# Attention's row-sum reciprocals on VectorE one unit later, without the round trip through memory, and key and value fetches moved into the first half of units

## The reference, cut to what matters

```python
h = _ada_ln(x, cond, Wln1, bln1)
q, k, v = heads(h @ Wq + bq), heads(h @ Wk + bk), heads(h @ Wv + bv)   # 16 heads of 32
scores = einsum('bhqd,bhkd->bhqk', q, k) / sqrt(32)
attn = softmax(scores, axis=-1)
x = x + einsum('bhqk,bhkd->bhqd', attn, v) @ Wo + bo
h = _ada_ln(x, cond, Wln2, bln2)
x = x + gelu(h @ W1 + b1) @ W2 + b2
```

## Time and profile before

| what | value |
|---|---|
| median of 3 runs | 3295.89 us (3295.88 to 3303.61) |
| the profiled execution's own time | 3315.78 us |
| its span, first to last instruction | 3314.2 us |
| mean granted TensorE clock | 0.978 |
| busy share of the span | PE 97%, DVE 63%, POOL 43%, ACT 42% |
| attention | about 378 to 2014 us, 32 units |

### The profile page before, as it was taken

How to read it: one execution, slowest core, us unless ns; L and a number is a source line. 1 busy time by engine, 2 the same in 40 slices (tenths; PEclk the granted TensorE clock), 3 DMA queues, 4 the chain that set the end, 5 groups by cost and what they waited for, 6 DMA issues and landing times.

```text
span 3314.2 us, 44368 instructions
## 1 busy us (share of the span) xinstructions
PE 3211.7 (97%) x16890; PEld 2200.4 (66%) x16890; DVE 2079.5 (63%) x3537; ACT 1391.1 (42%) x2703; POOL 1436.7 (43%) x656
## 2 busy tenths in 40 slices
PE   8798999999999999999999998899999999999999
PEld 7686655555555555555555545688888888778888
DVE  4647778778788787787878775543333332226766
ACT  2121366666666566665666663221111111012222
POOL 0200478778787786776867763210000000002222
PEclk9899999999999999999999999999999999889999
DMA  5474488888988788797887877520111112201221
GB/s 195 143 221 141 142 196 199 183 187 191 205 180 199 186 186 199 174 205 183 186 200 171 193 175 214 197 92 15 39 38 39 39 39 79 77 22 64 73 78 58
DMA packets 185883, 464.12 MB, mean 140 GB/s; under 512 B 27164, under 2 KB 69276, under 8 KB 154183
## 3 DMA queue, kind: packets, MB, share of 16 engines
q0 software_dynamic: 31968, 232.80, 31.5%
q1 hardware_dynamic: 153703, 228.49, 23.3%
HBM read 151.90 MB, written 75.76 MB: 69 GB/s over the span
## 4 chain that ended last, share of the span: by engine, by line
PE 86%; DMA 7%; DVE 3%; issue 2%; ACT 1%; POOL 1%; SPq 1%; DVEq 0%; POOLq 0%; ACTq 0%
PE ps L372 13%; PE ps L647 13%; PE ps L659 12%; PE ps L1178 11%; PE ps L1165 11%; DMA accd<-pt 5%; PE ps L446 4%; PE ps L1712 4%; PE ps L665 3%; PE ps L1725 3%; PE ps L450 2%; PE ps L1746 1%; PE ps L1541 1%; PE ps L1029 1%; DMA ao<-ao_d 1%
## 5 line engine op out<-in xcount | busy, mean ns | idle before, releaser
L385 DVE TENSOR_REDUCE nmp<-ps 128x1 f32<-128x512 f32 x1966 | 1202.2, 680 | 169.5 <-PE ps L372 168.1
L716 ACT ACTIVATE pt<-ps 128x512 f32<-128x512 f32 x2048 | 1033.4, 627 | 556.6 <-PE ps L647 556.5
L822 POOL TENSOR_TENSOR pacc<-pacc,pt 128x2048 f32<-128x2048 f32 x186 | 882.1, 4742 | 37.7 <-ACT pt L716 32.7
L647 PE MATMUL ps<-qs,ks 128*128 128x512 f32 x2048 | 817.3, 403 | 4.4 <-issue 4.0
L372 PE MATMUL ps<-ks,qs 96*128 96x512 f32 x1966 | 811.5, 413 | 3.3 <-POOL ones L798 3.3
L372 PEld LDWEIGHTS ps<-ks,qs 96*128 96x128 f32 x1966 | 377.8, 192 | 271.0 <-DVE nmp L385 162.7
L659 PE MATMUL ps<-pt,vq 128*32 128x512 f32 x4096 | 492.5, 598 | 0.0
L647 PEld LDWEIGHTS ps<-qs,ks 128*128 128x128 f32 x2048 | 393.8, 193 | 99.6 <-ACT pt L716 16.6
L1165 PE MATMUL ps<-hpb,w 128*128 128x512 f32 x1536 | 382.8, 399 | 3.4 <-DMA x_d<-x 3.4
L1178 PE MATMUL ps<-w,gp 128*128 128x512 f32 x1536 | 380.5, 396 | 2.3 <-DVE gp L1314 2.3
L1178 PEld LDWEIGHTS ps<-w,gp 128*128 128x128 f32 x1536 | 289.4, 188 | 71.7 <-DVE gp L1314 2.8
(11 more groups left out here) (175 smaller groups left out, 3180.9 us busy)
## 6 DMA issues: line engine op xcount, KB each, us to landing
accd<-pt POOLq DMA_DIRECT2D x222, 1024.0 KB, 9.1
qk_d<-st SPq DMA_DIRECT2D x128, 256.0 KB, 2.7
ks<-qk_d SPq DMA_DIRECT2D x24, 1024.0 KB, 16.0
qs<-qk_d SPq DMA_DIRECT2D x96, 256.0 KB, 6.8
xina<-in_x SPq DMA_DIRECT2D x8, 1024.0 KB, 6.4
v_d<-vst SPq DMA_DIRECT2D x32, 256.0 KB, 2.3
vq<-v_d SPq DMA_DIRECT2D x8, 1024.0 KB, 14.0
recb<-r_d SPq DMA_DIRECT2D x32, 256.0 KB
```

Of the source, the lines that this page charges most:

```text
L385: dve.tensor_reduce(nmp[:, n // 4, n % 4:n % 4 + 1], ps[:, ring.bank["max", u], :], AX.X, ALU.max, negate=True).then_inc(s_mr, 1)
L647: pe.matmul(ps[:, score_bank(n), :], ksb[w % 2][:, hh, 128 * kt:128 * kt + 128], qsb[:, v % 3, hh, :], start=True, stop=True).then_inc(s_s ...
L716: act.activation(pt[:, g % 8, hh, :], ps[:, score_bank(n), :], ACT.Exp, scale=SCALE).then_inc(s_exp, 1)
L822: pool.tensor_tensor(pacc[:, :, :], first, pt[:, g % 8, :, :], ALU.add).then_inc(s_add, 1)
```

## The change

The reciprocal's way through memory is taken out: sp_fold_sums, sp_store_recip, sp_load_recip, the tiles rs and rr and the buffer r_d are gone. VectorE copies the repeated sums of 128 x 512 to accs, which has two buffers, and takes the reciprocal of all 128 x 512 in place, one unit later: at the end of step 0 of unit v for unit v - 2. GpSimd multiplies behind its tile 2 of unit v, and SP stores at step 3. accv has two buffers too. In the last unit, unit 30's reciprocal is at step 3, its multiplication behind tile 10, and its store at step 6; unit 31's reciprocal stays at t = 2 of the output projection.

The keys are fetched in six DMAs of 512 KB in place of three of 1 MB, at steps 1, 3 and 4 of chunks 0 and 1, each held until the unit's scores have come to that step. The queries go out at step 2 under a wait that holds them until the scores of that step (before, they went out as soon as SP came to them). The values are fetched at step 4 of chunk 2, from a v_d whose layout now gives each partition one contiguous piece of 8 KB; the stores to v_d write pieces of 512 bytes where they wrote 2 KB. In the output projection x2 becomes one tile of five buffers, aT and boB lie elsewhere, and one wait for the end of attention is gone.

```diff
@@ -161,9 +161,8 @@
-    v_d = nc.dram_tensor("v_d", [B * S, D], F32, kind="Internal").ap()
+    v_d = nc.dram_tensor("v_d", [4 * B, 128, S // 128, 128], F32, kind="Internal").ap()
     ao_d = nc.dram_tensor("ao_d", [NT, 128, D], F32, kind="Internal").ap()
-    r_d = nc.dram_tensor("r_d", [2, 4, CH], F32, kind="Internal").ap()
...
-        accv = take("accv", [128, CH])
-        recb = take("recb", [128, CH])
+        accv = take("accv", [128, 2, CH])
+        accs = take("accs", [128, 2, CH])
         ones = take("ones", [128, 32])
-        rs = take("rs", [128, 16])
-        rr = take("rr", [128, 16])
...
-                pe.wait_ge(s_kd[w % 2], 48 * (w // 2 + 1))
+                pe.wait_ge(s_kd[w % 2], 96 * (w // 2 + 1))
...
 
-        def sp_load_k(w, r):
-            b, f, part = w // 4, 128 * (w % 4), (2, 3, 2)[r]
-            sp.dma_start(ksb[w % 2][32 * r:32 * r + 32, :, :].bitcast(F32),
-                         qk_d[b, part, f:f + 128, :].rearrange("(h e) s -> e h s", e=HD)).then_inc(s_kd[w % 2], 16)
+        def sp_load_k(w, r, half):
+
+            b, f, part = w // 4, 128 * (w % 4) + 64 * half, (2, 3, 2)[r]
+            sp.dma_start(ksb[w % 2][32 * r:32 * r + 32, 2 * half:2 * half + 2, :].bitcast(F32),
+                         qk_d[b, part, f:f + 64, :].rearrange("(h e) s -> e h s", e=HD)).then_inc(s_kd[w % 2], 16)
...
@@ -586,7 +584,8 @@
                             sp.wait_ge(s_qst[r], 128)
                         sp.wait_ge(s_pad, 3)
                     if ci == NCH and j in (1, 3, 5):
-                        sp_load_k(0, j // 2)
+                        sp_load_k(0, j // 2, 0)
+                        sp_load_k(0, j // 2, 1)
                     if ci == NCH and j in (6, 7):
                         sp_load_q(j - 6)
                     if ci == NCH + 2 and j == 0:
...
                     else:
-                        rows0 = CH * ci + 128 * (j - 8)
                         sp.wait_ge(s_vev, 4 * ci + j - 7)
-                        sp.dma_start(v_d[rows0:rows0 + 128, :], vst[:, j - 8, :]).then_inc(s_vst[j - 8], 16)
+                        sp.dma_start(v_d[4 * b:4 * b + 4, :, 4 * c + j - 8, :].rearrange("w p e -> p w e"),
+                                     vst[:, j - 8, :].rearrange("p (w e) -> p w e", w=4)).then_inc(s_vst[j - 8], 16)
...
@@ -717,9 +716,9 @@
 
         def act_values(v):
             act.wait_ge(s_pv, 16 * v + 16)
-            if v:
-                act.wait_ge(s_an, v)
-            act.activation(accv[:, :], ps[:, 7, :], ACT.Copy).then_inc(s_accv, 1)
+            if v >= 2:
+                act.wait_ge(s_an, v - 1)
+            act.activation(accv[:, v % 2, :], ps[:, 7, :], ACT.Copy).then_inc(s_accv, 1)
 
         def act_attention():
             qkv_over(act)
@@ -735,9 +734,13 @@
 
         def dve_sums(v):
             dve.wait_ge(s_end, v + 1)
-            if v:
-                dve.wait_ge(s_ao, 16 * v)
-            dve.tensor_copy(recb[:, :], ps[:, ring.bank["sums", v], :]).then_inc(s_accs, 1)
+            if v >= 2:
+                dve.wait_ge(s_ao, 16 * (v - 1))
+            dve.tensor_copy(accs[:, v % 2, :], ps[:, ring.bank["sums", v], :]).then_inc(s_accs, 1)
+
+        def dve_recip(v):
+            dve.wait_ge(s_accs, v + 1)
+            dve.reciprocal(accs[:, v % 2, :], accs[:, v % 2, :]).then_inc(s_rec, 1)
 
         def dve_add(kt):
 
@@ -755,12 +758,6 @@
             dve.wait_ge(s_wo, 16)
             dve.tensor_copy(wo[:, 0, k, :], wtmpo[:, k, :]).then_inc(s_wh, 1)
             dve_split(12 + k, wo[:, 1, k, :], wtmpo[:, k, :], wo[:, 0, k, :])
-
-        def dve_recip(v):
-            dve.wait_ge(s_rsd, 16 * (v + 1))
-            if v:
-                dve.wait_ge(s_rw, 16 * v)
-            dve.reciprocal(rr[:, :], rs[:, :]).then_inc(s_rec, 1)
 
         def dve_attention():
             qkv_over(dve)
@@ -779,7 +776,9 @@
                         dve_max(u)
                         if u % 64 == 63:
                             dve_row_max(u // 64)
-                if f == 2 and v:
+                if f == 0 and v >= 2:
+                    dve_recip(v - 2)
+                if f == 3 and v == NU - 1:
                     dve_recip(v - 1)
                 if v == NU - 1:
                     for kt in (2 * f, 2 * f + 1):
@@ -789,9 +788,9 @@
                         dve_out_turn(f - 5)
 
         def pool_values(v):
-            pool.wait_ge(s_recb, 16 * (v + 1))
+            pool.wait_ge(s_rec, v + 1)
             pool.wait_ge(s_accv, v + 1)
-            pool.tensor_tensor(recb[:, :], accv[:, :], recb[:, :], ALU.mult).then_inc(s_an, 1)
+            pool.tensor_tensor(accs[:, v % 2, :], accv[:, v % 2, :], accs[:, v % 2, :], ALU.mult).then_inc(s_an, 1)
 
         def pool_attention():
             qkv_over(pool)
@@ -820,39 +819,23 @@
                         pool.wait_ge(s_add, add_count(v, kt) - 1)
                         first = pacc[:, :, :]
                     pool.tensor_tensor(pacc[:, :, :], first, pt[:, g % 8, :, :], ALU.add).then_inc(s_add, 1)
-                if kt == 9 and v:
+                if kt == 2 and v >= 2:
+                    pool_values(v - 2)
+                if kt == 10 and v == NU - 1:
                     pool_values(v - 1)
 
         def sp_load_v(w):
-            b, f = w // 4, 128 * (w % 4)
-            sp.dma_start(vq[:, w % 2, :, :],
-                         v_d[S * b:S * b + S, f:f + 128].rearrange("(t p) e -> p t e", p=128)).then_inc(s_vq[w % 2], 16)
-
-        def sp_fold_sums(v):
-
-            sp.wait_ge(s_accs, v + 1)
-            if v:
-                sp.wait_ge(s_rec, v)
-            sp.dma_start(rs[:, :], recb[0:128:32, :].rearrange("h (c i) -> h c i", i=16)).then_inc(s_rsd, 16)
-
-        def sp_store_recip(v):
-            sp.wait_ge(s_rec, v + 1)
-            if v >= 2:
-                sp.wait_ge(s_recb, 16 * (v - 1))
-            sp.dma_start(r_d[v % 2].rearrange("h (c i) -> (h c) i", i=16), rr[:, :]).then_inc(s_rw, 16)
-
-        def sp_load_recip(v):
-
-            sp.wait_ge(s_rw, 16 * (v + 1))
-            sp.dma_start(recb[:, :], r_d[v % 2].unsqueeze(1).to_broadcast([4, 32, CH])).then_inc(s_recb, 16)
+            sp.dma_start(vq[:, w % 2, :, :], v_d[w]).then_inc(s_vq[w % 2], 16)
 
         def sp_store_ao(v):
             w, qc = divmod(v, NCH)
             b, k = divmod(w, 4)
             t0 = 16 * b + 4 * qc
             sp.wait_ge(s_an, v + 1)
+            if v:
+                sp.wait_ge(s_ao, 16 * v)
             sp.dma_start(ao_d[t0:t0 + 4, :, 128 * k:128 * k + 128].rearrange("s p r -> p s r"),
-                         recb[:, :].rearrange("p (s r) -> p s r", r=128)).then_inc(s_ao, 16)
+                         accs[:, v % 2, :].rearrange("p (s r) -> p s r", r=128)).then_inc(s_ao, 16)
 
         def sp_attention():
             qkv_over(sp)
@@ -860,24 +843,22 @@
             for p in range(NGRP // 2):
                 v, f = divmod(p, 8)
                 w, c = v // NCH + 1, v % NCH
-                if f == 1 and v:
-                    sp_fold_sums(v - 1)
                 if f == 2 and v >= 1 and v + 2 < NU:
-                    sp.wait_ge(s_sc, 64 * v)
+                    sp.wait_ge(s_sc, 64 * v + 16)
                     sp_load_q(v + 2)
-                if f == 3 and v:
-                    sp_store_recip(v - 1)
-                    sp_load_recip(v - 1)
+                if f == 3 and v >= 2:
+                    sp_store_ao(v - 2)
                 if f == 6 and v + 1 < NU:
                     sp_row(v + 1)
-                if f == 7 and v:
+                if f == 6 and v == NU - 1:
                     sp_store_ao(v - 1)
-                if v + NCH - c < NU and (c, f) in ((0, 6), (1, 4), (1, 7)):
+                if v + NCH - c < NU and c < 2 and f in (1, 3, 4):
+                    i = 3 * c + (1, 3, 4).index(f)
                     sp.wait_ge(s_pad, 5)
-                    if w >= 2:
-                        sp.wait_ge(s_sc, 256 * (w - 1))
-                    sp_load_k(w, ((0, 6), (1, 4), (1, 7)).index((c, f)))
-                if v + NCH - c < NU and (c, f) == (2, 7):
+                    sp.wait_ge(s_sc, 64 * v + 8 * f)
+                    sp_load_k(w, i // 2, i % 2)
+                if v + NCH - c < NU and (c, f) == (2, 4):
+                    sp.wait_ge(s_sc, 64 * v + 8 * f)
                     if w >= 2:
                         sp.wait_ge(s_pv, 64 * (w - 1))
                     sp_load_v(w)
@@ -905,15 +886,13 @@
         hpb0 = take("hpb0", [128, 2, NK, CH], F32R)
         b1c = take("b1c", [128, NF])
         after_f = cursor[0]
-        x2e = take("x2e", [128, D])
-        boB = place("boB", [128, D], chain_end - 6400)
+        boB = place("boB", [128, D], chain_end - 10368)
         wtb = place("wtb", [128, 3, D], after_w - 16384)
         cursor[0] = chain_end
         ao = take("ao", [128, 3, D])
-        x2 = take("x2", [128, 4, D])
-        aT = take("aT", [128, 2, 2, D], F32R)
+        x2 = take("x2", [128, 5, D])
+        aT = place("aT", [128, 2, 2, D], base + 16384, F32R)
```

(27 more changed lines are left out.)

## The result

The changed kernel takes 3266.27 us in the median of 4 runs (3262.93 to 3274.10), the kernel before 3297.02 beside it: ratio 0.9899, 95% interval 0.9876 to 0.9923. The forecast was 3256, its range 3243 to 3283. The three runs that the forecast started from lay low for the kernel before: in the later sets its median was 3303.0 (17 runs), 3304.7 (16) and 3304.1 (11), so by the medians the gain comes nearer 38 us than 31, and nearer the 39.7 of the sum. The profiled executions differ by more, 52.6 us of span.

The account below looks back on a forecast made before the run. PE, busy 97%, was taken to bound the kernel, losing time in attention to late accumulating DMAs. Terms -39.9 - 5.8 - 4 + 10 = -39.7 us took the median from 3295.9 to 3256 us, range 3243 to 3283.

Parts of the forecast that it names:

- the sum: Whole kernel: -39.9 (chunk 1 stalls) - 5.8 (Wo) - 4 (output projection) + 10 (keys) = -39.7 us.
- What bounds the kernel: Attention: PE, busy 97%, waits on late accumulating DMAs; 45.7 us lost in 30 units, 5.8 of it in unit 28.
- The reciprocal costs nothing: VectorE, end of step 0: 3.71 us for 512 elements fits the 3.96 us wait for the sums; cost 0.
- Rival B: VectorE, step 0: the reciprocal overruns its gap at 4.4 us, costing 9 us, 3265 us; chance 0.08.
- The cause of the stalls: Chunk 1: GpSimd's 4.95 us wait for recb and the third megabyte of keys delay tile 12's accumulate; 39.9 us.
- Keys, +10 us: Chunks 0 and 1: earlier key fetches cost 0.7 us in each of 14 units; bounds nothing to 42 us.
- tile 8's accumulate to land as late as in the chain: Chunks 0 and 1: some 16 us to landing, so GpSimd again issues tile 12 about 5 us late.
- Rivals A and C: Chunks 0 and 1, 14 units: A, backlog costs 1.5 to 3 us each (0.16); C, stall returns, 5.7 each (0.05).
- Wo, -5.8: Unit 28: Wo goes out some 9 us earlier, so the row of maxima behind it isn't late; bounds 0 and -5.8.
- Output projection, -4: After attention: tile fetch comes 5.8 us earlier, but VectorE spends 3.7 us on unit 31's reciprocal; bounds 0 and -7.
- The carry-over to the median: Whole kernel: the median lies 19.9 us below the profiled 3315.8, and the same difference is kept after the change.
- the backlog: Chunks 0 and 1: fetches pushed to each unit's front delay tile 8's and so tile 12's accumulate; 10 us.

Follow-up runs that it names:

- the first experiment: The changed kernel with keys, queries and values fetched where they were before, keeping the new reciprocal: 3259.63 us, ratio 0.9874.
- the second one of before: The kernel before, unchanged, profiled a second time: 3304.66 us in the median of 12 runs, ratio 1.0001; this profiled execution 3305.3 us.

## Why the prediction was right, and where its steps were not

- *What bounds the kernel: right.* The stalls of chunk 1, of the units behind them and of unit 28 were the gain: 45.5 us lost before, 0.1 after.
- *The reciprocal costs nothing: right, mis-sized on the safe side.* 3.34 us where 3.71 was worked out: 6.3 ns an element from the row of 16 on (3343 less 241 ns over 496), where 7.0 was taken. Rival B's 4.4 us did not come. By the Trainium skill (VectorE: DVE Perf Modes, "First, the fixed hardware budget", and the clock under "Specifications"), 8 repeats, if each takes a cycle at 0.96 GHz, make an estimate of over 4.27 us for 512 elements. The trace disagrees: 3.34 us. The cost of overrun, "nearly one for one", was right for the work, 2.7 us for 2.8, and left out the clock: 3.6 us in the mean. Rival B's 9 us took 0.3 us a unit for an overrun of 0.45, and no row gives that; one for one it would be 13.5.
- *The cause of the stalls: one link was missing.* The prediction put tile 12's late issue (38.1 us) down to the wait for recb. But tile 8's accumulate, for which tile 12's must wait, landed only 36.2 to 38.1 us into the units of chunk 1, and with the multiplication out of the way tile 12's still went out at 37.0 and later. The chain of the earlier trace rows says so, and the account of the causes left it out. The landing of tile 8's, issued at 20.9, follows what goes out just ahead of it: 6.9 to 7.7 us with nothing (chunk 3 of the first experiment), 10.6 to 12.0 with recb's load alone (chunk 3 before), 15.3 to 17.2 with recb's load and a megabyte of keys (chunk 1 before). The other cause, that the third megabyte of keys "goes out at 1079.56, just ahead of it", holds for tile 12's landing: 12.7 to 14.0 us with it ahead in the first experiment, 8.6 to 10.5 with it behind. Alone it does no harm, for a tile 12 that goes out at 32.5 still lands in time. The repeated load the sum had only as 1.2 us of engine work. The change takes out the wait, recb's load, and the keys' place ahead of tile 8 together; a megabyte of keys ahead of tile 8 without recb's load was not run.
- *Keys, +10 us: the term that was mis-sized.* It measured 0 in 13 of the 14 units and some 2.3 us in unit 0, which the sum counted like the others. The step that failed is "tile 8's accumulate to land as late as in the chain": in units 1 to 27 of chunks 0 and 1 it takes 8.9 to 11.3 us, not 16.4, and tile 12 goes out at 32.6 to 35.9 us, not 38.1. Rivals A and C rested on the same step.
- *Wo, -5.8: right in size, wrong in reason* (Wo held to its old place loses nothing).
- *Output projection, -4:* from the last copy of the sums to b2B it is 112.9 us (2081.3 less 1968.4) against 116.4, so -3.5. Other executions with the new reciprocal in its gap have 113.3 to 116.6, the second one of before 119.8, so the size is good to some 2 us. The 5.31 us idle of the earlier trace rows is gone, and waits of 0.6 to 2.7 us stand in its place.
- *The sum* by terms would have been -49.7 without the keys' +10; the profiled spans differ by 52.6: 2.2 ahead of attention's first score matmul, 43.9 in attention, 3.5 in the output projection, and 3.0 behind b2B. So the likeness of 49.7 and 52.6 is in part luck. *The carry-over to the median* was the weak link: the profiled execution of before lay at the top of its spread (3281 to 3316) and that of the changed kernel was the fastest of its first four. Two errors of some 8 and 10 us, the backlog that came in one unit only and the stall that most executions have less of, cancel, which is luck; most of the 10 us miss is then the low draw of the first three runs.
- *The fetches' half of the change* was counted as safe and useful. Beside the new reciprocal it gains nothing: unit 0's 2 us are its cost (0.9893, 0.9863 to 0.9924, in a second set, against 0.9874, 0.9851 to 0.9897, without it). By itself it costs 2%.

> The changed kernel, unchanged, with more rounds, to set it against the one that has only the new reciprocal (ratio 0.9874). If the new fetches cost something, it stays at 3266 and a ratio of 0.989 to 0.990; if the two differ only by the spread of executions, 3258 to 3263 and 0.987 to 0.988.

That second set of the changed kernel had a median of 3265.35 us (6 runs, 3258.38 to 3270.67). The 6 us between the two kernels aren't told apart by their intervals; their units 1 to 29 are the same, unit 0 explains some 2 us, and 15 of the 16 us between the two profiled spans lie behind b2B, where the clock was granted differently.

Open: why the repeated load is slow, and how the recovered time divides between it, GpSimd's wait and the times of the key DMAs. With unit 28 counted, moving the multiplication (and with it a key DMA) gave back 22 to 32 us of 36 to 46 in all, by a fast execution, and the load alone cost 23 beside the new fetches, so the shares overlap.

## What to carry to other kernels

A wait in an in-order queue is charged to everything behind it: before moving the transfers that seem to collide, look for the instruction that holds the queue when they are issued; and when it is moved, read again at what times the others go out, for they move too. A round trip of small dependent DMAs on the queue that also carries bulk loads gets longer with each load put ahead of it, so such a chain and early fetches are changed together or not at all. Compute that fills a gap in which its engine waits anyway is free to the end of the gap and costs one for one behind it, and more where the clock falls; and a delay read from the old trace should not be carried into a sum that takes its causes out. The first unit of a pipeline, where start-up work and early fetches meet, needs a look of its own: sums over the steady units leave it out.

## What the runs showed of the hardware that was not expected

- A DMA that reads four rows of 2 KB 32 times each slowed its neighbours: 256 KB a unit of it made Wo land in 25.1 us instead of 16.7 and cost 23 us in attention, while 256 KB of different rows cost nothing. Its landing was told by 5 semaphore updates, that of the different rows by 16.
- VectorE's reciprocal takes 241 ns for 16, 353 for 32, 1748 for 256 and 3343 for 512 elements a partition: 7.0 ns an element between the first two, 6.2 between the last two.
- One idle of PE of some 2 us in each unit was followed by the lower clock in two units of three (0.97 over the unit, 1.1 to 1.5 us lost) and not in the third.
- The same code was granted a clock of 0.90 or 0.98 over the 200 us in which the graph layer begins, worth some 15 us of the whole.
